# Gating a residual block: the second group's last VectorE step as (x - m)(1 + k s) + m, with small steps moved from ScalarE and TensorE to GpSimd

## What is computed

```python
x = x + _L0_conv_ref(_gn(x), ...)            # _gn: per group of 16 channels

# inside, for one group gx (16 x 128 x 128), already normalised
ch = _conv1x1(concat([mean(gx), max(gx)]), w_cc, b_cc)
channel_weight = sigmoid(_gn(ch, gn1_w, gn1_b))
hw = _conv1x1(concat([row means, column means]), w_s1, b_s1)
pos_h = sigmoid(_conv1x1(xh, w_ph, b_ph)); pos_w = sigmoid(_conv1x1(xw, w_pw, b_pw))
sx = conv3x3(gx * pos_h * pos_w, w_s3) + b_s3
spatial_weight = sigmoid(_gn(sx, gn2_w, gn2_b))
out = gx * (channel_weight * spatial_weight)
```

## Time and profile before

| | before |
|---|---|
| median of 3 runs | 3527.98 us (3526.47 to 3528.66) |
| profiled execution, time | 3526.81 us |
| profiled execution, span | 3524.7 us |
| DVE busy | 3421.2 us, 97% |
| PE busy | 3343.9 us, 95% |
| ACT busy | 2968.4 us, 84% |
| POOL busy | 1993.6 us, 57% |
| mean granted PE clock | 0.989 |

### The profile page before, as it was taken

How to read it: one execution, slowest core, us unless ns; L and a number is a source line. 1 busy time by engine, 2 the same in 40 slices (tenths; PEclk the granted TensorE clock), 3 DMA queues, 4 the chain that set the end, 5 groups by cost and what they waited for, 6 DMA issues and landing times.

```text
span 3524.7 us, 138640 instructions
## 1 busy us (share of the span) xinstructions
PE 3343.9 (95%) x52244; PEld 1601.2 (45%) x52244; DVE 3421.2 (97%) x1997; ACT 2968.4 (84%) x6274; POOL 1993.6 (57%) x907
## 2 busy tenths in 40 slices
PE   2999999999999999999999999999999999999996
PEld 1444444444444444444444444444444444444443
DVE  8899999999999999999999999999999999999995
ACT  2888888888888888888888888888888888888886
POOL 2566555655555565555566556556555655665562
PEclk9999999999999999999999999999999999999998
DMA  5466666666666667666666666666666666666654
GB/s 127 114 149 159 162 161 154 163 165 151 160 165 158 156 163 166 150 160 166 155 158 164 163 151 163 164 153 160 165 159 153 163 165 151 160 164 159 158 133 97
DMA packets 1115266, 547.03 MB, mean 155 GB/s; under 512 B 65712, under 2 KB 1114544, under 8 KB 1114544
## 3 DMA queue, kind: packets, MB, share of 16 engines
q1 hardware_dynamic: 836016, 403.05, 51.1%
q10 hardware_dynamic: 278528, 134.28, 13.8%
HBM read 268.63 MB, written 268.44 MB: 152 GB/s over the span
## 4 chain that ended last, share of the span: by engine, by line
DVE 33%; PE 29%; issue 22%; SPq 4%; ACT 3%; ACTq 3%; POOL 2%; DMA 2%; DVEq 0%; POOLq 0%
PE conv_ps L712 24%; DVE mx L624 8%; DVE sp_buf L579 7%; DVE sums L609 7%; DVE gated L664 4%; PE pos_ps L712 4%; SPq L240 4%; DVE fold L597 3%; ACTq L350 2%; DMA out<-sp_buf 2%; DVE sp_buf L589 2%; ACT sp_buf L361 2%; POOL rstd L301 1%; PE cw_ps L712 1%; POOL rstd L268 1%
## 5 line engine op out<-in xcount | busy, mean ns | idle before, releaser
L712 PE MATMUL conv_ps<-gated,W_conv 64*32 64x512 f32 x49152 | 2828.8, 593 | 56.4 <-ACT sp_buf L361 37.5
L712 PEld LDWEIGHTS conv_ps<-gated,W_conv 64*32 64x32 f32 x49152 | 1145.3, 106 | 1551.8 <-issue 1503.3
L287 POOL TENSOR_TENSOR gated<-gate_w,gate_hr 128x2048 f32<-128x2048 f32 x256 | 1175.1, 4590 | 20.2 <-POOL gate_hr L276 17.4
L361 ACT ACTIVATE sp_buf<-conv_ps,weights 128x512 f32<-128x512 f32 x1024 | 692.5, 677 | 207.5 <-DMA out<-sp_buf 120.4
L268 POOL TENSOR_TENSOR rstd<-var_e,consts 128x1 f32<-128x1 f32 x256 | 302.1, 1180 | 932.1 <-ACT var_e L398 932.1
L579 DVE SCALAR_TENSOR_TENSOR sp_buf<-xt,negm,sp_buf 128x2048 f32<-128x2048 f32 x256 | 600.3, 2345 | 30.1 <-ACT sp_buf L415 30.1
L589 DVE SCALAR_TENSOR_TENSOR sp_buf<-sp_buf,kfac,xt 128x2048 f32<-128x2048 f32 x256 | 602.1, 2352 | 9.0
L664 DVE SCALAR_TENSOR_TENSOR gated<-xt,negm,gated 128x2048 f32<-128x2048 f32 x256 | 591.2, 2351 | 14.2 <-POOL gated L287 14.2
L609 DVE TENSOR_REDUCE sums<-xt 128x32 f32<-128x4096 f32 x128 | 564.7, 4412 | 0.0
L624 DVE TENSOR_REDUCE mx<-xt 128x2 f32<-128x4096 f32 x128 | 564.3, 4408 | 0.0
L301 POOL TENSOR_TENSOR rstd<-var_e,consts 128x4 f32<-128x4 f32 x129 | 369.4, 2864 | 335.9 <-DVE var_e L651 335.9
(11 more groups left out here) (80 smaller groups left out, 1704.7 us busy)
## 6 DMA issues: line engine op xcount, KB each, us to landing
out<-sp_buf SPq DMA_DIRECT2D x2048, 128.0 KB, 2.5
xt<-in_x SPq DMA_DIRECT2D x1024, 128.0 KB, 3.4
xt<-in_x ACTq DMA_DIRECT2D x1024, 128.0 KB, 3.5
weights<-in_by_channel SPq DMA_DIRECT2D x1, 116.5 KB, 2.1
S_chan<-in_same_channel SPq DMA_DIRECT2D x1, 64.0 KB, 1.9
masks<-in_row_masks SPq DMA_DIRECT2D x1, 12.0 KB, 1.7
```

The lines of the kernel that those rows point to most:

```text
L287: nc.gpsimd.tensor_tensor(gated[:, d, j, 1:1 + NB, 1:1 + W], gate_w[:, d, j].unsqueeze(1).to_broadcast([P, NB, W]), gate_hr[:, d, j].unsqu ...
L361: nc.scalar.activation(sp_buf[:, g, k * BB:(k + 1) * BB], conv_ps[:, k], ACT.Identity, bias=V["b_s3"], accum_out=sums2).then_inc(evac, 1)
L712: return nc.tensor.matmul(ps, lhsT, rhs, start=start, stop=stop)
```

## The change

Four edits, with what belongs to them:

1. For the second group, ACT turns the gate s into 1 + k s in place (`gate_plus_one`, a 2048-element activation behind the sigmoid), DVE's `gate_x` waits for that and gives (x - m)(1 + k s), and DVE's last step is `add_mean`, a `tensor_scalar` that adds m back, in place of `add_x`, a `scalar_tensor_tensor`. The first group is finished as before.
2. The third halving of the columns (4 blocks to 2) is a new `fold_columns` on POOL; `positions` on PE then needs two matmuls for the columns in place of four.
3. Of the channel norm, ACT keeps the two instructions that read PSUM (`channel_in`, now after eviction 2) and the sigmoid. The difference, the square, the sum with epsilon (`channel_variance`, between the two `rstd2_power`) and the last product (`channel_norm`, first in the turn) are on POOL, one instruction of 2 elements each, each waiting for the one ahead of it.
4. On ACT, b's last eviction stands ahead of `gates`.

```diff
+            def fold_columns(u):                       # POOL
+                pool.wait_ge(fold4_done, u + 1)
+                if later(u, 1):
+                    pool.wait_ge(pos_mm, u)
+                nc.gpsimd.tensor_tensor(fold2[:], fold4[:, :, 0:2], fold4[:, :, 2:4], ALU.add).then_inc(fold2_done, 1)
+            def channel_variance(u, s):                # POOL
+                pool.wait_ge(ch_in, 2 * u + 2)
+                if later(u, 1):
+                    pool.wait_ge(ch_norm, u)
+                nc.gpsimd.tensor_tensor(ch[:, 1], ch[:, 0], ch[:, 0], ALU.subtract).then_inc(ch_var, 1)
+                pool.wait_ge(ch_var, 3 * u + 1)
+                nc.gpsimd.tensor_tensor(ch[:, 2], ch[:, 1], ch[:, 1], ALU.mult).then_inc(ch_var, 1)
+                pool.wait_ge(ch_var, 3 * u + 2)
+                if later(u, 1):
+                    pool.wait_ge(rstd_done, u)
+                nc.gpsimd.tensor_tensor(var_e[:, (s + 1) % 2, 2:4], ch[:, 2], consts[:, 4:6],
+                                        ALU.add).then_inc(ch_var, 1)
+            def channel_norm(u, s):                    # POOL
+                pool.wait_ge(rstd_done, u + 2)
+                if later(u, 1):
+                    pool.wait_ge(cgate_done, u)
+                nc.gpsimd.tensor_tensor(ch[:, 3], ch[:, 1], rstd[:, (s + 1) % XS, 2:4], ALU.mult).then_inc(ch_norm, 1)
...
+            def gate_plus_one(u, s, j):                # ACT
+                flat = sp_buf[:, 2 * (s % 2) + j].rearrange("p b w -> p (b w)")
+                act.wait_ge(sig2, 2 * u + j + 1)
+                act.wait_ge(kfac_done, u + 1)
+                nc.scalar.activation(flat, flat, ACT.Identity, scale=kfac[:, s, j:j + 1],
+                                     bias=consts[:, 8:9]).then_inc(one_plus, 1)
...
                 if real(b):
                     spatial_gate(b, sb_, 1)
+                    gate_plus_one(b, sb_, 1)
...
                 dve.wait_ge(sig2, n + 1)
+                if j == 1:
+                    dve.wait_ge(one_plus, u + 1)
...
+            def add_mean(u, s, j):                     # DVE
+                dve.wait_ge(fin_a, 2 * u + j + 1)
+                nc.vector.tensor_scalar(flat, flat, negm[:, s, j:j + 1], None, ALU.subtract).then_inc(final, 1)
...
                     gate_x(b, sb_, 1)
-                    add_x(b, sb_, 1)
+                    add_mean(b, sb_, 1)
...
-                        for i in range(4):
-                            mm(pos[:, :, NB:NB + W], W_cols[:, :], fold4[:, :, i], start=i == 0, stop=False)
+                        for i in range(2):
+                            mm(pos[:, :, NB:NB + W], W_cols[:, :], fold2[:, :, i], start=i == 0, stop=False)
```

More of the change, by code:

```diff
@@ L149, in conv_attention @@
         fin_a = sem("fin_a")
+        one_plus = sem("one_plus")
         final = sem("final")
@@ L152, in conv_attention @@
         ch_mm = sem("ch_mm")
+        ch_in = sem("ch_in")
         ch_var = sem("ch_var")
@@ L314, in body @@
                 c, sc = t + 2, (q + 2) % XS
+                if real(t):
+                    channel_norm(t, q)
                 if real(a):
@@ L321, in body @@
                     gate_products(a, sa, 1)
+                if real(c):
+                    fold_columns(c)
                 if real(b):
                     rstd2_power(b, sb_, 0)
+                if real(a):
+                    channel_variance(a, sa)
                 if real(b):
@@ L441, in gates, with channel_in @@
                                          scale=rstd[:, s, j:j + 1], bias=b_pos[:, 1:2]).then_inc(gates_done, 1)
-            def channel_variance(u, s):
+            def channel_in(u, s):
                 act.wait_ge(ch_mm, u + 1)
                 if later(u, 1):
-                    act.wait_ge(cgate_done, u)
+                    act.wait_ge(ch_var, 3 * u)
                 for j in range(2):
                     nc.scalar.activation(ch[:, 0, j:j + 1], cw_ps[:, j:j + 1], ACT.Identity,
-                                         scale=rstd[:, s, j:j + 1], bias=V["b_cc"]).then_inc(ch_var, 1)
-                for j in range(2):
-                    act.wait_ge(ch_var, 6 * u + j + 1)
-                    nc.scalar.activation(ch[:, 1, j:j + 1], ch[:, 0, j:j + 1], ACT.Identity, scale=-1.0,
-                                         bias=ch[:, 0, j:j + 1]).then_inc(ch_var, 1)
-                act.wait_ge(ch_var, 6 * u + 4)
-                nc.scalar.activation(ch[:, 2], ch[:, 1], ACT.Square).then_inc(ch_var, 1)
-                act.wait_ge(ch_var, 6 * u + 5)
-                if later(u, 1):
-                    act.wait_ge(rstd_done, u)
-                nc.scalar.activation(var_e[:, (s + 1) % 2, 2:4], ch[:, 2], ACT.Identity,
-                                     bias=consts[:, 4:5]).then_inc(ch_var, 1)
-            def channel_gate(u, s):
-                act.wait_ge(rstd_done, u + 2)
-                for j in range(2):
-                    nc.scalar.activation(ch[:, 3, j:j + 1], ch[:, 1, j:j + 1], ACT.Copy,
-                                         scale=rstd[:, (s + 1) % XS, 2 + j:3 + j]).then_inc(ch_norm, 1)
-                act.wait_ge(ch_norm, 2 * u + 2)
+                                         scale=rstd[:, s, j:j + 1], bias=V["b_cc"]).then_inc(ch_in, 1)
+            def channel_gate(u, s):
+                act.wait_ge(ch_norm, u + 1)
                 if later(u, 2):
@@ L502, in body @@
                     evacuate(t, q, 2)
+                if real(a):
+                    channel_in(a, sa)
                 if real(b):
@@ L508, in body @@
                     evacuate(t, q, 4)
-                if real(a):
-                    channel_variance(a, sa)
                 if real(t):
```

25 lines of the change are left out of this document (15 added, 10 removed).

## The result

The changed kernel takes 3609.18 us (median of 4 runs, 3593.46 to 3620.59) against 3527.22 (3525.45 to 3528.66) for the kernel before: a ratio of 1.023, 95% interval 1.019 to 1.027. It is slower, where the prediction said 3419 and gave the slower side 0.22; 3609 also lies outside the range of 3395 to 3535. The profiled execution took 3603.31, its span is 3601.2 and its mean granted clock 0.967 (0.989 before).

A forecast was written before the change was run, and what follows sets the result against it. DVE was taken as the bound: 26.77 - 2.27 + 1.17 = 25.67 us a turn, plus 0.2 stall, 25.87; 0.90 saved over 121 turns takes 109 us off, giving 3419 us, range 3395 to 3535.

The forecast's parts named there:

- The short turn, 25.67: DVE's turn of 26.77 us with add_x, 2.27, replaced by a tensor_scalar of 1.17.
- D: Rival on DVE: add_mean misses the double rate or POOL blocks its gain; 3520 to 3530 us; chance 0.08.
- The halving, 1.05: POOL's new column halving of 512 elements: 1.05 us, bounds 0.90 to 1.43.
- C: Rival on POOL: halving over 1.1, second power always misses add_x; all turns 27.6, 3628 us; chance 0.18.
- The first channel step: First of POOL's three small channel-norm steps: slightly late for the free stretch, let in at modulate's end, 11.6 into the turn.
- its last place: Second group's power on POOL, issued 0.02 ahead of DVE's add_x: passes, or the second gate_x is 1.9 late.
- The stall of 0.2 a turn for slow stores: ACT's 1 + k s late for DVE's second gate_x after slow stores: 0.2 us a turn, bounds 0 and 0.5.
- B: Rival: turns alternate, POOL's power missing its place after slow stores; mean turn 26.63, 3511 us; chance 0.22.
- A: Likeliest case: every turn short, 25.87 us, 109 us saved, 3419 us (3395 to 3455); chance 0.50.
- PE's own turn falls ... to about 24.9 and stays below 25.67: PE, two matmuls fewer in positions: its turn falls from 25.66 us and stays under DVE's.
- The swap costs POOL nothing: ACT's gates behind eviction 7: delay hidden by the last DVE step; without that cover, gates and products 0.7 us later.
- E: Rival: a POOL product gets in ahead of add_mean, DVE waits 3.61 each turn; 3830 us; chance 0.02.

The follow-up runs named there:

- e12: Changed kernel with all its edits, PE's hardware loop unrolled to 24 turns in place of 6: 3437.58 us, ratio to the kernel before 0.975.
- e1: Changed kernel with 16 idle matmuls on PE ahead of its loop, putting the loop's start back in its old place: 3499.8 us, ratio to before 0.992.
- e5: Changed kernel with 16 idle matmuls ahead of PE's loop and ACT's gates ahead of eviction 7 again: 3480.89 us, ratio to before 0.987.
- e4: Kernel before with only ACT's 1 + k s and DVE's add_mean for the second group: 3487.92 us, ratio to before 0.988.
- e10: Changed kernel with ACT's gates ahead of eviction 7 again and PE's loop unrolled to 24 turns: 3430.78 us, ratio to before 0.973.
- e6: Changed kernel with ACT's gates ahead of eviction 7 again, no idle matmuls: 3550.96 us, ratio to before 1.007.
- e7: Changed kernel with 48 idle matmuls ahead of PE's loop and ACT's gates ahead of eviction 7 again: 3471.3 us.

## Why the prediction was wrong, point by point

- **The short turn, 25.67**: right. 25.74 in the turn shown, 25.63 in many others. The tensor_scalar takes 1.29 for 1.25; D is out. ACT's 1 + k s takes 2.10, as said. `positions` shrank from 2.71 to 1.87 (said: 1.9).
- **The halving, 1.05**: mis-sized, 1.28 where nothing blocks it, within the bounds 0.90 to 1.43. By the text that was C's condition (over 1.1, every turn 27.6, 3628 us). It did not come to that, and that the measured 3609 lies near C's 3628 is chance. POOL's timeline of the same turn, which answers to the earlier trace rows:

```profile
1631.13 1.29 POOL L302 TENSOR_TENSOR fold<-fold 128x512 f32<-128x512 f32 x1
1632.37 0.56 POOL L273 TENSOR_TENSOR rstd<-var_e,consts 128x1 f32<-128x1 f32 x1
1632.88 0.20 POOL L309 TENSOR_TENSOR ch<-ch 128x2 f32<-128x2 f32 x1
1633.16 2.12 POOL L311 TENSOR_TENSOR ch<-ch 128x2 f32<-128x2 f32 x1
1635.36 2.18 POOL L315 TENSOR_TENSOR var_e<-ch,consts 128x2 f32<-128x2 f32 x1
1638.12 2.04 POOL L273 TENSOR_TENSOR rstd<-var_e,consts 128x1 f32<-128x1 f32 x1 [0.57 <-ACT var_e L437]
```

  The first channel step is issued at 1632.88, 0.02 behind modulate, and passes in 0.20. The two others are let in at the ends of the two modulates, as the text had it, so the second power comes a DVE instruction before its last place and ends at 1640.16, ahead of ACT's need for it (1640.28). Where a slow store makes the steps later, it does stand at that place, and passes: in e12's timelines of POOL and DVE it is issued 0.03 ahead of add_x.

```profile
1319.89 0.55 POOL L273 TENSOR_TENSOR rstd<-var_e,consts 128x1 f32<-128x1 f32 x1
```
```profile
1319.92 2.35 DVE L624 SCALAR_TENSOR_TENSOR sp_buf<-sp_buf,kfac,xt 128x2048 f32<-128x2048 f32 x1
```

- **The stall of 0.2 a turn for slow stores**: right. In e12 it is 21.1 us in 30 waits, 0.18 a turn, the longest 1.2 (said: up to 1.4). B did not come.
- **A's sum**: right once the pause is out of the way. e12 has 25.98 a turn over 121 turns (162.75 to 3306.38) for 25.87, and 3437.6 us, 19 above 3419 and within A's range of 3395 to 3455.
- **"PE's own turn falls ... to about 24.9 and stays below 25.67"**: this is the step that failed. 24.9 is right for a turn without a jump: after the change PE's shortest turns take 25.2, with 0.3 of waiting in them. One turn in six also holds the jump, and the text took PE's cost from a turn of the chain in which none lay. Before, the pause of 2.2 to 2.9 cost 0.3 to 0.4 a jump (27.05 against 26.69), since PE had about a us a turn to spare; it stood in the trace as a wait for "issue" with a longest of 2.8, and I read over it. The text then took that cost as unchanged, without saying so. Two things made it large. Edit 2 moved the loop's start to a bad place (5.2 to 6.2 in place of 2.2 to 2.9). And with the shorter turn the other engines absorb even the short pause no longer: it costs 3.6 a jump in e1 and 3.1 in e5 (29.29 and 28.76 against 25.7), and 1.8 with edit 1 alone (e4, 27.52). How that cost is shared among the engines no run separates.
- **"The swap costs POOL nothing ... If that cover goes, the gates are 0.7 later"**: half failed. Where PE is on time, edit 4 costs at most about 7 us (e12 against e10, 0.2%, inside the 0.3% that the expectation called level). The cover goes at each jump, and then it is not 0.7 but the whole of eviction 7's wait for PE, 7.59 in the turn shown. This alone is 58 of the changed kernel's us (e6).
- **The rivals**: none held a cost outside the turn that was costed. Both that ended on the slower side, C and E, were worked out inside the same turn, and neither came: in e12, with few pauses, the mean turn is 25.98, and only three of 121 take over 29, at the three jumps.
- **The chances**: A's 0.50, B's 0.21 and D's 0.02 make 0.73 and not 0.72; nothing hangs on it.

The sum that the runs give for the 82 us: short turns, -109 by the prediction's A and -90 as measured with few pauses (e12); the loop's place, +109 (e1 against after) with edit 4 as it is, and the short pauses, which now show, +62 (e1 against e12). -90 + 62 + 109 = 81. The three add up by construction, each being the difference of two runs; what they show is the size of each. The 4 us by which e1's idle matmuls delay the start make the 109 smaller and the 62 larger.

## What to carry to other kernels

Removing instructions ahead of a hardware loop moves the loop in its engine's instruction stream, and the jump back can then cost twice as much: look for idle time released by "issue" once per loop pass, and cost the turn that holds the jump by itself. Before you make the other engines' turn shorter, ask whether the engine with the jump still catches up; if not, unroll more or shift the loop's start by a few idle instructions and look again. Don't put a wait for an engine that pauses ahead of work that others need early (here eviction 7 ahead of the gates).

## What was not expected of the hardware

- The pause of TensorE at a jump back has two lengths, 2.2 to 3.3 and 5.2 to 6.9 us, by the place of the loop modulo 256 instructions; the second 16 KiB instruction packet begins within the long pause and behind the short one. At one place in between (e7) the pause is short, and a second stop of up to 1.59 us follows 31 matmuls later.
- After the long pause the granted clock is at the lower level for some us: in the turn shown it is 0.50 over the next 4.5 us, and 36 matmuls take 125 ns each, where 59 is usual. Behind the short pause 144 matmuls took 10.00 before and, at 59 ns each, would take 8.4, so the short pause costs some of this too: the granted clock there is 0.64 from 1683.3 to 1688.0.
- A POOL step of two elements that was issued 0.02 behind the start of a DVE instruction with two SBUF inputs still passed in 0.20. At 1606.46 one passed 0.05 behind the modulate of 1606.41. A product of 2048 elements issued 0.08 behind took 5.75 in place of 3.61.
- The halving of 512 elements with two SBUF inputs takes 1.28 alone, 2.5 ns an element, where the product of 2048 takes 1.8 ns an element (3.61).
